# GpSimd's split of a later batch's context, moved from between the fourth and fifth sums of exponentials to behind a batch's last sum

## The chip, the cores and the metric

One core of one Trainium2 chip runs the whole program. The metric is the device time of one execution in microseconds (us), lower being better; the value given for a kernel is the median of its runs.

## The reference

The inputs are 32 sequences of 256 tokens with 256 features, and for each a context of 256 tokens. The reference applies three blocks, each followed by `x = layernorm(x + block(x))`:

```python
x = _layernorm(x + _L0_attn_ref(x, ...))             # 4 layers: sLSTM over 256 steps + feed-forward
x = _layernorm(x + _L0_xattn_ref(x, ctx_1024, ...))  # cross-attention, 16 heads of 64
x = _layernorm(x + _L0_ffn_ref(x, ...))              # ternary weights, 8-bit activations
...
def _L0_xattn_ref(x, context, mask, Wq, Wkv, Wo, bo):
    q = x @ Wq
    k, v = jnp.split(context @ Wkv, 2, axis=-1)
    sim = jnp.einsum('bhid,bhjd->bhij', q, k) * SCALE
    sim = jnp.clip(jnp.where(mask, sim, max_neg), -5.0, 5.0)
    attn = jax.nn.softmax(sim, axis=-1)
    out = jnp.einsum('bhij,bhjd->bhid', attn, v)
    return out @ Wo + bo
```

The change lies in the part that computes the cross-attention and the last feed-forward block. The context enters only through `k` and `v`.

## The kernel before, in words

The kernel has two stages. The first (`slstm`, to about 2220 us of the profile) runs the recurrence. The second (`attend_and_feed`) runs over 32 batches `j`, one sequence each. Every engine has its own list of instructions for the whole stage, written out by hand in program order, and works through it in that order; semaphores alone tie the lists together.

For each batch TensorE first computes 12 units of keys, queries and values (`unit`, L835 for keys and queries, L842 for values), and between them the first half of the feed-forward block of the batch before (`transpose_x`, L920; `feed_in`, L938). Inputs and weights are held as two fp16 numbers, a high part and the rest, and each product is three matmuls. Then come four quads of four heads each. For quad `q` TensorE computes scores of pairs of heads (`scores`, L857), exponentials times values (`attend`, two halves, L867), and the sums of the exponentials (`denominators`, L879); from the second quad on it also multiplies the quad before by `Wo` (`out_project`, L911, 6 matmuls for a pair of heads). Behind the last quad come the last two pairs of `out_project`. `transpose_h` (L948) and `feed_out` (L957) of the batch before stand in quads 2 and 3.

VectorE clips the scores (`clip`, L1175, two heads at a time, into the buffer `scores`), divides (`attended`, L1260), writes the low parts of keys and queries (L1246), quantises (`round_up`, L1227: `gate<-hidden_f`; `round_down`, L1231: `hidden_quant<-gate`), and prepares the x of batch j+2 in pieces: `x1_moments` (L1287, L1290), `x1_centre` (L1296), `x1_residual` (L1305), `x1_second_norm` (L1315, two instructions, one for each half of the tokens). In each batch `attended` of quad 0 is followed by the `round_up` of the second half of the tokens, and then by the clips of heads 8 and 9; `attended` of quad 3 follows `x1_second_norm`; then come `last_attended_lo` (L1267), `fed` (L1273) and `x_plus_attended` (L1463). ScalarE takes the exponentials (L1027), the high parts (L1059, L1063, L1080, L1090) and the logarithm and exponential of the denominators (L1071, L1073).

GpSimd has this list for a batch `j`: `add_halves` for each of 16 heads (L771), which adds the exponentials of the two halves of the context and waits for ScalarE's exponentials of that head; between the fourth and the fifth of them `context_split(j + 2)`; `attended_lo` of quads 0, 1 and 2 (L775) behind heads 7, 11 and 15; in batch 0 alone `below_half` (L780, part of the ternary weights) behind heads 5, 9 and 13; and last `residual(j + 2)` (L765), which waits for VectorE's `x_plus_attended` of batch j. `context_split(n)` waits for the load of batch n and for all 12 units of batch n-2, whose slot it writes; then it writes the high part of the context (L757, a cast) and the low part (L759, a subtraction) into `batch_inputs_hi` and `batch_inputs_lo`. TensorE waits for both only at unit 0 of batch n (`in_split`).

The DMA queue of SyncE loads batch n (`load`, L725 to L728) once `in_split` of batch n-2 and `x1_step` of batch n-1 have come; in its list this load stands behind the store of the result of batch n-4.

The two waits of TensorE that GpSimd can end are these:

```python
def denominators(j, q):
    pe.wait_ge(halves_added, 4 * (n + 1))
def out_project(j, pair):
    pe.wait_ge(ot_split, QUADS * j + pair // 2 + 1)
```

Of the kernel before, what the change touches and what calls it, by code (L numbers as in the profile page):

```python
# [15 lines left out]
B, S, D = 32, 256, 256  # L16
# [569 lines left out]
def attend_and_feed(nc, ctx, a, x4, out, kept):  # L586
# [128 lines left out]
    with nc.Block() as block:  # L715

        @block.sync
        def _(sp):
            def load(n):

                i = n % SLOTS
                if n >= SLOTS:
                    sp.wait_ge(x1_step, X1_OPS * (n - 1))
                    sp.wait_ge(in_split, 2 * (n - 1))
                sp.dma_start(x4t[:, i], token_rows(x4, FIRST, n)).then_inc(in_loaded[i], DMA)  # L725
                if n >= SLOTS:
                    sp.dma_start(xt[:, i], token_rows(a["x"], 0, n)).then_inc(in_loaded[i], DMA)
                    sp.dma_start(cb[:, i], a["ctx"][:, :, n]).then_inc(in_loaded[i], DMA)  # L728

            def store(f):  # L730

                if f > 0:
                    sp.wait_ge(out_stored, f * STORE)
                sp.sem_inc(result_free, 1)
                for tt in range(QT):
                    sp.wait_ge(res_done, f * QT + tt + 1)
                    sp.dma_start(out[f:f + 1, tt * P:(tt + 1) * P, :].rearrange("o t d -> t (o d)"),
                                 res[:, f % SLOTS, tt]).then_inc(out_stored, DMA)

            load(0)  # L740
            load(1)
            for j in range(B):
                if j + 2 < B:
                    load(j + 2)
                if j > 0:
                    store(j - 1)
            store(B - 1)
            sp.wait_ge(out_stored, B * STORE)

        @block.gpsimd  # L750
        def _(pool):
            def context_split(n):
                i = n % SLOTS
                pool.wait_ge(in_loaded[i], LOADS2 * DMA * (n // SLOTS + 1))
                if n > 1:
                    pool.wait_ge(unit_ready, UNITS * (n - 1))
                nc.gpsimd.tensor_copy(xc_hi[:, i, 1], cb[:, i]).then_inc(in_split, 1)  # L757
                pool.wait_ge(in_split, 2 * n + 1)
                nc.gpsimd.tensor_tensor(xc_lo[:, i, 1], cb[:, i], xc_hi[:, i, 1], ALU.subtract).then_inc(in_split, 1)  # L759

            def residual(n):
                pool.wait_ge(x1_step, X1_OPS * (n + 1))
                if n > 1:
                    pool.wait_ge(xa_done, QT * (n - 1))
                nc.gpsimd.tensor_tensor(x1b[:, n % SLOTS], x1[:], bo[:, None, :].broadcast_to([P, QT, D]), ALU.add).then_inc(x1_bo_done, 1)  # L765

            def add_halves(j, i):
                pool.wait_ge(exp_done, AHEADS * j + i + 1)
                if QUADS * j + i // 4 > 1:
                    pool.wait_ge(den_ready, QUADS * j + i // 4 - 1)  # L770
                nc.gpsimd.tensor_tensor(psum[:, i % RING, :], pr[:, i % RING, 0:S], pr[:, i % RING, S:2 * S], ALU.add).then_inc(halves_added, 1)  # L771

            def attended_lo(j, q):
                pool.wait_ge(ot_hi_done, QUADS * j + q + 1)
                nc.gpsimd.tensor_tensor(ot_lo[:, 2 * q:2 * q + 2, :], ot[:, q % 2], ot_hi[:, 2 * q:2 * q + 2, :],  # L775
                                        ALU.subtract).then_inc(ot_split, 1)

            def below_half(m):
                pool.wait_ge(ff_op, 3)
                nc.gpsimd.tensor_scalar(ff_t[:, m, :], ff_raw[:, m, :], ff_minus_half[:, m:m + 1], None, ALU.is_lt).then_inc(ff_below, 1)  # L780

            context_split(0)
            nc.gpsimd.memset(onesf[:], 1.0).then_inc(ones_ready, 1)
            nc.gpsimd.memset(onesb[:], 1.0).then_inc(ones_ready, 1)
            pool.wait_ge(ones_ready, 2)
            for i_, o_ in ((identf, onesf), (identb, onesb)):
                nc.gpsimd.affine_select(out=i_[:], in_=o_[:], compare_op=ALU.is_equal, fill=0.0, base=0,
                                        pattern=[[1, P]], channel_multiplier=-1).then_inc(ident_ready, 1)
            context_split(1)
            pool.wait_ge(w_loaded, DMA * kept["loads"])  # L790
            residual(0)
            residual(1)
            pool.wait_ge(wo_split, 2)
            for j in range(B):
                for i in range(AHEADS):
                    add_halves(j, i)
                    if i == 3 and j + 2 < B:
                        context_split(j + 2)
                    if i % 4 == 3 and i > 3:
                        attended_lo(j, i // 4 - 1)  # L800
                    if j == 0 and i % 4 == 1 and i > 3:
                        below_half(i // 4 - 1)
                if j + 2 < B:
                    residual(j + 2)

        @block.tensor
# [726 lines left out]
```

## Time and profile before

| | before |
|---|---|
| median of 3 runs | 3738.53 us (3736.28 to 3739.94) |
| the profiled execution, its own time | 3732.63 us |
| span of the profiled execution | 3730.9 us |
| granted TensorE clock, mean | 0.99 |
| TensorE busy | 3615.0 us (97%) |
| VectorE busy | 3460.5 us (93%) |
| ScalarE busy | 3064.7 us (82%) |
| GpSimd busy | 2253.7 us (60%) |

The profile is of one execution. Times in it are from the start of the span. In a timeline a row is one instruction or several alike in a row (xcount), its first number is the start and its second the duration of all of them; in square brackets stands how long the engine was idle before it and who ended that. PE is TensorE's matmuls and PEld its weight loads, DVE is VectorE, ACT ScalarE and POOL GpSimd.

### The profile page before, as it was taken

Reading aid. Unit: us, or ns where it says so; the run is one execution under the profiler, and the core shown is the slowest. Engines: PE = TensorE matmul, PEld = TensorE weight load, DVE = VectorE, ACT = ScalarE, POOL = GpSimd, SP = SyncE. Lnnn points to the kernel's source line nnn. Section 1 sums busy time; section 2 is a strip of 40 time slices with the busy share of each in tenths; the row PEclk is TensorE's granted clock in tenths of the full one; section 3 lists DMA queues with packets and bytes.
Section 4 is the critical chain, followed back from the end, with each engine's and each line's share of the span. In section 5 each row is a group of like instructions: output and inputs, shape, how many; then the busy total and the mean of one; then the engine's idle time right before and its main releaser. Section 6 shows DMA issues by size and latency. Waiting matters only on the chain. (4 is left out here: it accounts for less than half of the span.)

```text
span 3730.9 us, 167466 instructions
## 1 busy us (share of the span) xinstructions
PE 3615.0 (97%) x71481; PEld 2282.1 (61%) x71481; DVE 3460.5 (93%) x9241; ACT 3064.7 (82%) x6357; POOL 2253.7 (60%) x2395
## 2 busy tenths in 40 slices
PE   6999999999999999999999987999999999999997
PEld 3666666665666666666666654666666666666664
DVE  8999999999999999999999987889988898888886
ACT  4999999999999999999999984677776677777675
POOL 3777777777777777777777764444444444444442
PEclk9999999999999999999999998999999999999998
DMA  2000221000000000000000000000000000100000
GB/s 82 25 25 25 56 59 53 25 25 25 25 25 25 25 25 25 25 25 25 25 25 25 25 26 18 24 24 24 24 24 24 24 24 28 32 24 24 24 16 10
DMA packets 99973, 104.27 MB, mean 28 GB/s; under 512 B 17297, under 2 KB 95005, under 8 KB 98729
## 3 DMA queue, kind: packets, MB, share of 16 engines
q1 hardware_dynamic: 99224, 93.56, 8.7%
q8 instruction: 560, 9.18, 1.0%
q14 instruction: 189, 1.54, 0.1%
HBM read 48.52 MB, written 17.53 MB: 18 GB/s over the span
## 5 line engine op out<-in xcount | busy, mean ns | idle before, releaser
L565 POOL TENSOR_TENSOR conv_products<-normed_features,conv_taps_by_token 128x256 f32<-128x256 f32 (+1 forms) x837 | 757.9, 919 | 530.2 <-ACT normed_features L348 530.1
L771 POOL TENSOR_TENSOR exps_of_both_halves<-scores 128x256 f32<-128x256 f32 x512 | 424.2, 851 | 583.8 <-ACT scores L1027 578.4
L295 PE MATMUL banks<-up_centred,after_cell_features 128*32 128x336 f32 x8928 | 740.3, 449 | 1.1 <-ACT after_cell_features L348 0.5
L295 PEld LDWEIGHTS banks<-up_centred,after_cell_features 128*32 128x32 f32 x8928 | 260.5, 109 | 277.6 <-issue 224.1
L302 PE MATMUL banks<-down,hidden_features 112*32 112x256 f32 x6696 | 419.2, 383 | 0.0
L578 POOL TENSOR_TENSOR conv_partial_sums<-conv_products,conv_partial_sums 128x512 f32<-128x512 f32 x279 | 370.5, 1328 | 21.9
L1027 ACT ACTIVATE scores<-scores 128x512 f32<-128x512 f32 x512 | 305.4, 626 | 77.7 <-DVE scores L1175 74.0
L366 ACT ACT_TABLE_LOAD x279 | 358.0, 1283 | 5.2
L381 ACT ACT_TABLE_LOAD x279 | 358.0, 1283 | 5.1
L1175 DVE SCALAR_TENSOR_TENSOR scores<-banks,score_top 128x512 f32<-128x512 f32 x512 | 327.9, 681 | 26.1 <-PE banks L857 25.5
L269 PE MATMUL banks<-recurrent_weights,h_features 64*32 64x256 f32 x8928 | 313.1, 379 | 0.3 <-DVE h_features L509 0.2
L867 PE MATMUL banks<-scores,v_tokens 128*32 128x256 f32 x4096 | 274.0, 385 | 11.9 <-ACT scores L1027 11.7
L579 POOL TENSOR_TENSOR conv_partial_sums<-conv_products,conv_partial_sums 128x256 f32<-128x256 f32 x279 | 265.1, 950 | 0.0
L302 PEld LDWEIGHTS banks<-down,hidden_features 112*32 112x32 f32 x6696 | 189.0, 109 | 121.3
L571 POOL TENSOR_TENSOR conv_partial_sums<-conv_products,conv_partial_sums 128x256 f32<-128x256 f32 x279 | 220.3, 790 | 65.9 <-DVEq L466 44.0
L835 PE MATMUL banks<-batch_inputs_hi,qkv_weights_hi 128*128 128x256 f16 x1024 | 196.0, 273 | 11.3 <-POOL batch_inputs_lo L759 9.8
L269 PEld LDWEIGHTS banks<-recurrent_weights,h_features 64*32 64x32 f32 x8928 | 196.1, 106 | 8.3 <-DVE h_features L509 1.5
L835 PE MATMUL banks<-batch_inputs_lo,qkv_weights_hi 128*128 128x256 f16 x1024 | 196.0, 273 | 0.0
L835 PE MATMUL banks<-batch_inputs_hi,qkv_weights_lo 128*128 128x256 f16 x1024 | 195.9, 273 | 0.0
L867 PEld LDWEIGHTS banks<-scores,v_tokens 128*32 128x32 f32 x4096 | 120.9, 110 | 107.6 <-ACT scores L1027 27.1
L269 PE MATMUL banks<-gate_weights,convolved_features 64*32 64x128 f32 x8928 | 186.2, 275 | 0.0
L503 DVE SCALAR_TENSOR_TENSOR convolved_features<-tanh_half_conv,conv_partial_sums 128x256 f32<-128x256 f32 x279 | 180.0, 645 | 0.5 <-ACT tanh_half_conv L365 0.5
(222 smaller groups left out, 9933.3 us busy)
## 6 DMA issues: line engine op xcount, KB each, us to landing
layer_inputs<-layer_outputs SPq DMA_DIRECT2D x279, 96.0 KB, 2.0
layer_inputs<-in_x SPq DMA_DIRECT2D x280, 32.0 KB, 1.8
x_scratch<-layer_outputs SPq DMA_DIRECT2D x279, 32.0 KB
x_tokens<-in_x SPq DMA_DIRECT2D x32, 256.0 KB, 3.0
context_features<-in_ctx SPq DMA_DIRECT2D x32, 256.0 KB, 3.7
layers_out<-x_scratch SPq DMA_DIRECT2D x32, 256.0 KB, 2.8
out<-result SPq DMA_DIRECT2D x64, 128.0 KB, 1.8
up_centred<-in_ff_up SPq DMA_DIRECT2D x1, 2688.0 KB
```

Source lines behind the costliest of these rows:

```text
L269: mm = nc.tensor.matmul(bank[group(l), 2 * (j % 2) + odd, at + g0 * DH:at + g1 * DH], src[r, n, group(l)], w[r, l, n, g0:g1, :].rearrange( ...
L295: mm = nc.tensor.matmul(bank[group(l), b, 0:UP], xmt[:, n, group(l)], up[:, l, n, at:at + UP], start=n == 0, stop=n == HALF - 1, skip_grou ...
L302: mm = nc.tensor.matmul(bank[group(l), FD, 0:D], hidt[:, i, group(l)], down[:, l, i, :], start=i == 0, stop=i == UTILES - 1, skip_group_ch ...
L366: nc.scalar.preload_act_table_set(LOG_EXP)
L381: nc.scalar.preload_act_table(ACT.Gelu)
L565: return nc.gpsimd.tensor_tensor(prod[:, i:i + n], xnt[:, j % NRING].rearrange("p n t -> p (n t)")[:, None, :].broadcast_to([P, n, HALF * ...
L578: nc.gpsimd.tensor_tensor(new[:, 0:2], prod[:, 0:2], old[:, 1:3], ALU.add).then_inc(conv_done, 1)
L771: nc.gpsimd.tensor_tensor(psum[:, i % RING, :], pr[:, i % RING, 0:S], pr[:, i % RING, S:2 * S], ALU.add).then_inc(halves_added, 1)
L835: mm = nc.tensor.matmul(bank[:, b, i * S:(i + 1) * S], w_[:, m, h, (2 * n + i) * P:(2 * n + i + 1) * P], x_[:, j % SLOTS, src, h, :], star ...
L867: mm = nc.tensor.matmul(bank[32 * g:32 * g + 32, b, at:at + S], stationary(kt, i), pr[:, i % RING, kt * S:(kt + 1) * S], start=kt == 0, st ...
L1027: nc.scalar.activation(pr[:, i % RING, :], pr[:, i % RING, :], ACT.Exp, scale=S_SCALE).then_inc(exp_done, 1)
L1175: nc.vector.scalar_tensor_tensor(out=pr[:, i % RING, :].rearrange("p (k s) -> p k s", k=KT), in0=bank[:, i % SCORES, :].rearrange("p (k s) ...
```

## The change

GpSimd's call of `context_split(j + 2)` leaves its place between `add_halves(j, 3)` and `add_halves(j, 4)` and stands behind the whole loop over the heads, ahead of `residual(j + 2)`. Its two instructions and its waits are the same. It is called in the same 30 batches (j = 0 to 29); in batches 30 and 31 it is called in neither kernel.

```diff
             for j in range(B):
                 for i in range(AHEADS):
                     add_halves(j, i)
-                    if i == 3 and j + 2 < B:
-                        context_split(j + 2)
                     if i % 4 == 3 and i > 3:
                         attended_lo(j, i // 4 - 1)
                     if j == 0 and i % 4 == 1 and i > 3:
                         below_half(i // 4 - 1)
                 if j + 2 < B:
+                    context_split(j + 2)
                     residual(j + 2)
```

## Rows read from the trace of the kernel before

**Rows 1.** The page: the chain that ended last, shares by engine

```profile
PE 33%; DVE 4%; ACT 2%; issue 1%; POOL 0%; DMA 0%; DVEq 0%; POOLq 0%
```

**Rows 2.** Chain that ended last, pieces of 60 key and query matmuls: start us, us, what

```profile
3564.73 6.55 PE banks L835 x60
...
3609.51 6.55 PE banks L835 x60
...
3654.48 6.55 PE banks L835 x60
```

**Rows 3.** Waits, 3563 to 3608 (batch 29): us in total, times, longest us

```profile
PEld banks L879 <- POOL exps_of_both_halves L771: 0.2, 1, 0.2
...
PEld banks L911 <- POOL attended_lo L775: 0.4, 1, 0.4
```

**Rows 4.** Timeline of GpSimd, batch 16: start us, us, engine line op, shapes, xcount [idle before]

```profile
3004.97 0.61 POOL L757 CAST batch_inputs_hi<-context_features 128x512 f16<-128x512 f32 x1
...
3005.66 1.49 POOL L759 TENSOR_TENSOR batch_inputs_lo<-context_features,batch_inputs_hi 128x512 f16<-128x512 f32 x1
...
3020.12 1.35 POOL L775 TENSOR_TENSOR attended_lo<-attended,attended_hi 128x512 f16<-128x512 f32 x1
...
3027.70 1.27 POOL L765 TENSOR_TENSOR x_plus_bo<-x_tokens,bo 128x512 f32<-128x512 f32 x1 [6.23 <-DVE x_plus_attended L1463]
```

**Rows 5.** Timeline of VectorE, the same batch

```profile
3007.81 0.69 DVE L1260 TENSOR_TENSOR attended<-banks,denominator_log 128x512 f32<-128x512 f32 x1 [0.23 <-ACT denominator_log L1073]
...
3008.42 0.74 DVE L1227 TENSOR_SCALAR gate<-hidden_f,quant_scale 128x1024 f32<-128x1024 f32 x1
...
3009.08 1.28 DVE L1175 SCALAR_TENSOR_TENSOR scores<-banks,score_top 128x512 f32<-128x512 f32 x2
...
3021.97 0.74 DVE L1315 TENSOR_SCALAR x_tokens<-x_tokens,x_mean_var,x_rstd 128x256 f32<-128x256 f32 x2 [0.64 <-ACT x_rstd L1086]
...
3022.68 0.69 DVE L1260 TENSOR_TENSOR attended<-banks,denominator_log 128x512 f32<-128x512 f32 x1
...
3024.07 0.69 DVE L1267 TENSOR_TENSOR attended_lo<-attended,attended_hi 128x512 f16<-128x512 f32 x1 [0.70 <-ACT attended_hi L1080]
```

**Rows 6.** Timeline of TensorE, the same batch

```profile
3015.43 0.28 PE L857 MATMUL banks<-q_hi,k_hi 64*128 64x256 f16 x2 [0.17 <-DVE scores L1175]
...
3025.29 0.27 PE L911 MATMUL banks<-wo_hi,attended_hi 128*128 128x256 f16 x1
```

**Rows 7.** Groups of VectorE by line and form, 2357 to 3607: busy us, mean ns

```profile
L1227 DVE TENSOR_SCALAR gate<-hidden_f,quant_scale 128x1024 f32<-128x1024 f32 x56 | 42.6, 760 | 0.0
```

**Rows 8.** Timeline of GpSimd, batch 30, which has no split

```profile
3635.84 0.72 POOL L771 TENSOR_TENSOR exps_of_both_halves<-scores 128x256 f32<-128x256 f32 x1 [1.22 <-ACT scores L1027]
```

**Rows 9.** Timeline of VectorE and (last row) TensorE, batch 30

```profile
3635.33 0.69 DVE L1260 TENSOR_TENSOR attended<-banks,denominator_log 128x512 f32<-128x512 f32 x1 [0.23 <-ACT denominator_log L1073]
...
3635.94 1.18 DVE L1227 TENSOR_SCALAR gate<-hidden_f,quant_scale 128x1024 f32<-128x1024 f32 x1
...
3637.03 1.27 DVE L1175 SCALAR_TENSOR_TENSOR scores<-banks,score_top 128x512 f32<-128x512 f32 x2
...
3637.77 0.28 PE L857 MATMUL banks<-q_hi,k_hi 64*128 64x256 f16 x2 [0.36 <-DVE scores L1175]
```

**Rows 10.** Timeline of VectorE and (last row) GpSimd in batch 0: operations that overlap

```profile
2291.70 1.38 DVE L1296 SCALAR_TENSOR_TENSOR layers_out<-layers_out,x_mean_var,post_scale 128x256 f32<-128x256 f32 x1
...
2302.45 1.05 DVE L1315 TENSOR_SCALAR x_tokens<-x_tokens,x_mean_var,x_rstd 128x256 f32<-128x256 f32 x1 [0.60 <-ACT x_rstd L1086]
...
2291.41 1.38 POOL L775 TENSOR_TENSOR attended_lo<-attended,attended_hi 128x512 f16<-128x512 f32 x1
```

**Rows 11.** Timeline of GpSimd and (last row) TensorE in batch 0

```profile
2271.85 0.60 POOL L757 CAST batch_inputs_hi<-context_features 128x512 f16<-128x512 f32 x1
...
2273.64 1.42 POOL L771 TENSOR_TENSOR exps_of_both_halves<-scores 128x256 f32<-128x256 f32 x2
...
2281.92 1.08 PE L879 MATMUL banks<-exps_of_both_halves,ones_for_sums 128*32 128x256 f32 x8 [4.50 <-POOL exps_of_both_halves L771]
```

## The prediction

> **What bounds the kernel now.** I began with the chain that ended last. TensorE holds 33% of it against 4% for VectorE and none for GpSimd [rows 1], and in the second stage it goes through TensorE from batch to batch: one batch begins 44.78 us behind the other [rows 2]. So a change on GpSimd counts only where it moves TensorE. Next I read the waits of one batch. TensorE's list waits for GpSimd at two places, the sums of quad 1 and the first low part of the attended values, for 0.2 and 0.4 us [rows 3], and both are weight loads that stood still while their matmul row had no idle time of its own. Then I laid the timelines of the three engines of batch 16 side by side. GpSimd spends from 3004.97 to 3007.15 on the split [rows 4]. At the end of the batch it has nothing to do for 6.23 us until the residual, which waits for VectorE [rows 4]. VectorE has no idle time from 3007.81 to the second norm at 3021.97 [rows 5], and TensorE waits for it at 3015.43 [rows 6]. Within a batch the score part is thus a loop of TensorE and VectorE, and each tenth that VectorE loses between 3007.81 and 3015.4 goes to TensorE.
>
> **What is moved.** Two GpSimd instructions, 0.69 us from start to start and 1.49 for the second (2.2 us together), in 30 batches; no DMA and no work is added. The queues it passes: the context load of batch j+2 was issued a batch earlier, and the next load that waits for the split stands in SyncE's list behind a store of a later batch, so no transfer moves; its reader on TensorE comes more than a batch later. Behind the new place stands only the residual. The split would run from about 3021.4 (end of the last low part, 3020.12 + 1.35) to about 3023.5, and the residual starts at 3027.70 [rows 4]: it is hidden there, and costs GpSimd's own list nothing. If that cover went, it would cost up to 2.2 us a batch.
>
> **What the old place gives back.** The sums of heads 4 to 7 run when their exponentials come. TensorE gains at most its two waits, 0.6 us a batch [rows 3]; I take nothing, because no matmul stood idle for them.
>
> **Term 1, the sums in their new time.** GpSimd and VectorE hold each other up where VectorE reads two operands from SBUF or runs a scalar operation there: the same 128x256 scalar instruction that takes 0.37 us (0.74 for two) [rows 5] took 1.05 in batch 0, where GpSimd was at a low part [rows 10]. So it matters which pairs meet. Batch 30 has no split, and up to its first `attended` it is what every batch becomes. Counted from that `attended`, VectorE's clips of heads 8 and 9 begin 1.27 us later in batch 16 (3007.81 to 3009.08) [rows 5] but 1.70 us later in batch 30 (3635.33 to 3637.03) [rows 9]. Between them stands `gate<-hidden_f`: 0.74 us with the split [rows 5], 1.18 without [rows 9], because a sum of GpSimd has begun 0.10 us before it [rows 8]. In 28 batches with the split the 56 instructions of this form have a mean of 760 ns [rows 7], so none is held up. TensorE pays at once: its scores of heads 10 and 11 wait 0.36 us in batch 30 [rows 9]. Batch 30 lasts 44.97 us, 0.19 longer than batch 29, though VectorE has no x of a later batch to prepare [rows 2]. In batches 1 to 29 VectorE stays busy until the clip for which TensorE waits at 3015.43, so nothing takes the loss up: 29 x 0.43 = 12.5 us. Bounds: 0.36 us (TensorE's wait in batch 30) to 0.6 (should another instruction meet a sum), 10 to 17 us.
>
> **Term 2, the split in its new time.** No batch shows a split there, so I use the nearest overlap. VectorE's second norm is two scalar instructions at 3021.97 and about 3022.3 [rows 5]. The split's low part is ready 0.69 us behind the cast's start at about 3021.43, at 3022.12: between the two. In batch 0 a low part of the same size became ready at 2291.41, and the second instruction of a pair, from 2291.70, took 1.38 us [rows 10]. I take the second norm's second instruction as held so: 1.3 for 0.37, 0.95 us more. `attended` of quad 3 (3022.68) and `last_attended_lo` (3024.07 to 3024.76) [rows 5] go back with it, the latter to an end at 3025.71. TensorE's matmul that needs it stands at 3025.29 [rows 6]: 0.53 us of slack are used up and about 0.45 remain. 29 x 0.45 = 13 us. Bounds: nothing, if the low part comes after both instructions; and 1.1 us a batch, if both are held (0.7 us more by the other row, 1.05 against 0.37 [rows 10]): 0 to 32 us. The middle is taken since the same size of GpSimd instruction and the same pair of VectorE did this.
>
> The Trainium skill says in its page "SBUF — State Buffer", section "SBUF: two separate sides", that the port pair which VectorE and GpSimd share is a lock that whoever starts first holds for its whole instruction. This trace lets go sooner: VectorE's instruction ends at 2293.08, only 0.29 us behind the end of GpSimd's at 2292.79 [rows 10]. By the page, the second norm would end a whole 0.37 us behind the low part, some 0.1 us more a batch, and the sum would come to 28 us.
>
> **Batch 0.** There GpSimd is the bound: TensorE stood 4.50 us before the sums of quad 1 [rows 11]. The sums of heads 4 and 5 can begin where the cast did, 1.8 us earlier (2271.85 for 2273.64) [rows 11]. At the end of the batch the split meets VectorE's x and its last ternary weights, and most of this may be lost: -1.8 to 0, I take -0.5.
>
> **Sum.** 12.5 + 13 - 0.5 = 25 us. The profiled execution of before took 3732.6 us, 0.16% under the median of the runs, and would take 3757.6; against the median, 3763.5.
>
> **Rivals.**
> Only term 1: GpSimd's low part slips behind both instructions of the second norm, or the slack of 0.53 us holds. For it: 0.18 us later is enough to slip. Against it: both overlaps of rows 10 held VectorE. 3738.5 + 12 = 3750.5 us.
> Both terms larger: both instructions of the second norm are held, 12.5 + 32 - 0.5 = 44, 3782.5 us. The first starts 0.07 us before the cast's end, so it could be.
> Nothing moves: the waits that appear have slack that I missed. Against it: the wait of 0.36 us in batch 30. 3738 us.
> Faster: VectorE's loop gains. The split goes from beside `hidden_quant` ahead of 3007.81, GpSimd lags less, and if `gate<-hidden_f` isn't caught, TensorE's wait at 3015.43 (0.17 us) goes, 5 us in 29 batches, with 1.8 in batch 0: 3731.7 us. It decides from the point where the sum of head 6 begins over 0.1 us later than in batch 30, behind `gate<-hidden_f`.
> That the change doesn't do what it says can't be here: GpSimd's list runs in the written order.
>
> **How the numbers follow.** The forecast has 0.62, only term 1 0.18, larger 0.06, nothing 0.09, faster 0.05. A measurement of this kernel can tell about 0.2%, 7.5 us, from no change; both the forecast and the case of term 1 alone lie above it. Faster 0.05, same 0.09, slower 0.86. The range goes from the case of term 1 alone to the forecast with some of term 2's upper bound: 3749 to 3772.
>
> **What would show it.** `gate<-hidden_f` of the second half at 1.18 us in batches 1 to 29, and the mean of the 56 at about 970 ns; TensorE idle 0.36 us before the scores of heads 10 and 11; the second norm's pair at about 1.7 us for 0.74; TensorE waiting about 0.45 us for VectorE before `out_project` of pair 6; 45.65 us from batch to batch, and 1.8 us less at the sums of quad 1 in batch 0. A period of 45.2 would leave term 2 wrong, one of 44.8 or less the whole argument.

## The result, and the profile after

| | before | after |
|---|---|---|
| median | 3737.7 us (4 runs) | 3755.0 us (4 runs, 3752.9 to 3756.5) |
| the profiled execution | 3732.6 us | 3755.1 us |
| from batch to batch, most batches | 44.78 us | 45.52 us |

The change makes the kernel slower: the ratio of after to before is 1.0045 (95% interval 1.0028 to 1.0063), 17 us. In the code of after all lines behind the moved call stand one line earlier (L1227 is now L1226, L1315 is L1314, and so on).

The page of after, its first line and the chain by engine; TensorE's share was 33% [rows 1]:

```profile
span 3753.3 us, 167466 instructions
...
PE 27%; DVE 6%; ACT 4%; issue 3%; POOL 0%; DMA 0%; DVEq 0%; POOLq 0%
```

The chain that ended last, in order of time (start us, us, what), where batches 29, 30 and 31 begin:

```profile
3586.76 6.55 PE banks L834 x60
...
3632.27 6.55 PE banks L834 x60
...
3677.24 6.55 PE banks L834 x60
```

Batch 29 lasts 45.51 us where it lasted 44.78; batch 30, in which neither kernel splits a context, lasts 44.97 in both [rows 2]. So the loss is in the batches with a split, and is the same in each: from batch 2 on they last 45.51 to 45.53 us, but for batch 13, which is 0.35 us longer in both kernels. In the kernel before one batch, number 28, lasted 45.38 us (more on it below).

The timeline of VectorE in batch 16, the rows that answer to [rows 5] (start us, us, engine, line, operation, shapes, xcount, idle before):

```profile
3020.82 0.69 DVE L1259 TENSOR_TENSOR attended<-banks,denominator_log 128x512 f32<-128x512 f32 x1 [0.23 <-ACT denominator_log L1072]
...
3021.43 1.18 DVE L1226 TENSOR_SCALAR gate<-hidden_f,quant_scale 128x1024 f32<-128x1024 f32 x1
...
3022.53 1.27 DVE L1174 SCALAR_TENSOR_TENSOR scores<-banks,score_top 128x512 f32<-128x512 f32 x2
...
3035.41 1.58 DVE L1314 TENSOR_SCALAR x_tokens<-x_tokens,x_mean_var,x_rstd 128x256 f32<-128x256 f32 x2 [0.64 <-ACT x_rstd L1085]
...
3036.91 0.68 DVE L1259 TENSOR_TENSOR attended<-banks,denominator_log 128x512 f32<-128x512 f32 x1
...
3038.28 0.69 DVE L1266 TENSOR_TENSOR attended_lo<-attended,attended_hi 128x512 f16<-128x512 f32 x1 [0.70 <-ACT attended_hi L1079]
```

`gate<-hidden_f` takes 1.18 us for 0.74, and the clips behind it begin 1.71 us after `attended` for 1.27: 0.44 us lost. The pair of the second norm takes 1.58 us for 0.74: 0.84 us lost. The second instruction of the pair by itself:

```profile
3035.74 1.25 DVE L1314 TENSOR_SCALAR x_tokens<-x_tokens,x_mean_var,x_rstd 128x256 f32<-128x256 f32 x1
```

GpSimd's timeline of the same batch:

```profile
3021.33 1.87 POOL L771 TENSOR_TENSOR exps_of_both_halves<-scores 128x256 f32<-128x256 f32 x2 [1.22 <-ACT scores L1026]
...
3034.86 0.61 POOL L757 CAST batch_inputs_hi<-context_features 128x512 f16<-128x512 f32 x1
...
3035.55 1.29 POOL L759 TENSOR_TENSOR batch_inputs_lo<-context_features,batch_inputs_hi 128x512 f16<-128x512 f32 x1
...
3041.45 1.27 POOL L765 TENSOR_TENSOR x_plus_bo<-x_tokens,bo 128x512 f32<-128x512 f32 x1 [4.61 <-DVE x_plus_attended L1462]
```

The sums of heads 6 and 7 now begin 0.10 us ahead of `gate<-hidden_f` (3021.33 against 3021.43), as in batch 30 of the kernel before [rows 8]. The split's cast starts at 3034.86, its low part at 3035.55, between the two instructions of the second norm (3035.41 and 3035.74), and the second of them ends at 3036.99, 0.15 us behind the low part's own end. The residual still waits 4.61 us for VectorE: in GpSimd's own list the split is hidden. The context load that SyncE issues in this batch comes 10.96 us after the batch's start, where it was 10.98 before, so it didn't move.

TensorE's timeline of the same batch, its two waits for a clip and the two matmuls on either side of its new wait:

```profile
3023.26 0.28 PE L856 MATMUL banks<-q_hi,k_hi 64*128 64x256 f16 x2 [0.37 <-DVE scores L1174]
...
3028.87 0.28 PE L856 MATMUL banks<-q_hi,k_hi 64*128 64x256 f16 x2 [0.17 <-DVE scores L1174]
...
3038.62 0.27 PE L910 MATMUL banks<-wo_hi,attended_lo 128*128 128x256 f16 x1
...
3039.03 0.28 PE L910 MATMUL banks<-wo_hi,attended_hi 128*128 128x256 f16 x1
```

It waits 0.37 us before the scores of heads 10 and 11, where batch 16 of before had no wait, then 0.17 as before [rows 6]. The last two rows are the end of pair 5 and the start of pair 6 of `out_project`: 0.41 us apart where two matmuls in a row stand 0.11 apart, so 0.30 us lost. With the 0.44 us that the clips come later this makes the 0.74 of the period.

The groups by line and form from batch 2 to 29 (busy us, mean ns, idle before):

```profile
L1226 DVE TENSOR_SCALAR gate<-hidden_f,quant_scale 128x1024 f32<-128x1024 f32 x56 | 54.0, 965 | 0.0
...
L1314 DVE TENSOR_SCALAR x_tokens<-x_tokens,x_mean_var,x_rstd 128x256 f32<-128x256 f32 x56 | 44.1, 830 | 17.9 <-ACT x_rstd L1085 17.9
```

The mean of `gate<-hidden_f` went from 760 [rows 7] to 965 ns, that of the second norm from 410 to 830: every batch is alike.

Batch 0 in before: the residual of batch 1 on GpSimd's timeline, which shows how late the second stage was, and the start of batch 1 in the chain. Below it the same two rows of after, and between them TensorE's first matmuls of the sums of quad 1:

```profile
2267.86 1.27 POOL L765 TENSOR_TENSOR x_plus_bo<-x_tokens,bo 128x512 f32<-128x512 f32 x1 [24.56 <-DVE x_tokens L1315]
...
2309.95 6.55 PE banks L835 x60
```

```profile
2268.59 1.27 POOL L765 TENSOR_TENSOR x_plus_bo<-x_tokens,bo 128x512 f32<-128x512 f32 x1 [23.31 <-DVE x_tokens L1314]
...
2280.85 0.64 PE L878 MATMUL banks<-exps_of_both_halves,ones_for_sums 128*32 128x256 f32 x8 [2.74 <-POOL exps_of_both_halves L771]
...
2310.38 7.99 PE banks L834 x60
```

This execution of after came 0.73 us later into batch 0 (2268.59 for 2267.86), and still had the sums of quad 1 1.07 us earlier (2280.85 for 2281.92 [rows 11]), so the freed place gave 1.8 us. At the start of batch 1 it was 0.43 us later (2310.38 for 2309.95), and 0.73 of lateness less 0.43 leaves 0.3 us of the gain, by one profile of each kernel. Then the first 60 matmuls took 7.99 us for 6.55. Stretches of 2310 to 2318 us, busy time of each engine, then the granted clock (0.80) and DMA; first before, then after:

```profile
2310.00:2318.00 8.00, 8.00 (x76) 7.08 (x74) 7.47 (x22) 4.97 (x10) 1.27 (x1) 1.00 0.00 0
```

```profile
2310.00:2318.00 8.00, 8.00 (x61) 6.59 (x60) 5.96 (x19) 4.06 (x7) 1.27 (x1) 0.80 0.00 0
```

The 0.80 is a mean: TensorE was granted 0.50 (1.2 GHz) from 2310 to 2312 us, 0.70 from 2312 to 2314 and 1.00 (2.4 GHz) from then on, where the kernel before had 1.00 throughout. In both kernels it had stood idle for over 5 us before the last sums of batch 0 (5.41 us, and 5.14 before). The experiments show below that this loss comes and goes.

### The profile page after: what moved, and what is told of

Read it like the earlier page. It is cut to its first block and busy times, and to the rows that moved or that the text cites. A ratio compares the mean times of both kernels' runs of the same rounds, so it can differ in the third digit from the quotient of the medians.

```text
span 3753.3 us, 167466 instructions
## 1 busy us (share of the span) xinstructions
PE 3623.8 (97%) x71481; PEld 2280.2 (61%) x71481; DVE 3486.8 (93%) x9241; ACT 3064.8 (82%) x6357; POOL 2256.6 (60%) x2395
## 5 line engine op out<-in xcount | busy, mean ns | idle before, releaser
L771 POOL TENSOR_TENSOR exps_of_both_halves<-scores 128x256 f32<-128x256 f32 x512 | 431.9, 864 | 649.5 <-ACT scores L1026 646.2
```

## The experiments

The theory was that two overlaps of GpSimd and VectorE cost: a sum that now holds `gate<-hidden_f`, and the split's low part that holds the second norm. I give the time from batch to batch for most batches from the chain of each profile, since it repeats to 0.01 us, and the ratio to the kernel before of the same chip beside it. Chips differ: the kernel before had medians of 3731.95, 3737.73 and 3730.68 us on the three chips on which most of the experiments ran.

### The split behind the residual

```diff
                 if j + 2 < B:
-                    context_split(j + 2)
                     residual(j + 2)
+                    context_split(j + 2)
```

> The changed kernel with the split one step later, behind the residual. Theory (two overlaps cost: a sum of GpSimd holds VectorE's gate<-hidden_f 0.43 us, and the split's low part holds the second norm 0.84 us, of which 0.53 are slack): the second goes, the first stays. gate<-hidden_f still 1.18 us, the second norm's pair back at 0.74, no wait of TensorE before out_project of pair 6, 45.2 us from batch to batch (45.52 in the changed kernel, 44.8 before), about 3746 us. Rival (the split delays the residual and with it the batch's end): the residual is now ahead, all is back, 44.8 and 3738 us. Rival (the split costs wherever it stands ahead of a batch's first sum): 45.5, 3755 us.

Measured: 45.44 us from batch to batch, ratio 1.0050 (1.0034 to 1.0067). This is a miss: the second norm is free, but the batch is only 0.08 us shorter than in the changed kernel, close to the second rival's 45.5. The starts of batches 3 and 4 in the chain, and the groups of `x2` (written `x`) and of the second norm:

```profile
2397.74 6.55 PE banks L834 x60
...
2443.18 6.55 PE banks L834 x60
...
L1189 DVE TENSOR_SCALAR x<-x_plus_attended,mean_var,rstd 128x256 f32<-128x256 f32 x52 | 40.7, 825 | 0.0
...
L1314 DVE TENSOR_SCALAR x_tokens<-x_tokens,x_mean_var,x_rstd 128x256 f32<-128x256 f32 x52 | 19.1, 411 | 16.6 <-ACT x_rstd L1085 16.6
```

The second norm is back at 411 ns, but `x` of the batch before, a pair of the same kind that takes 405 ns in the other kernels, now takes 825: the split meets it at the start of the next batch. The kind of overlap is that of the theory, but I had not looked at what stands at the place to which I moved the split. The pair is held for 0.84 us as the second norm was, and 0.22 us of it reach the period (45.44 against the 45.22 of the next experiment). They do so at two waits of TensorE's weight loads, for `x_quant` and for `hidden_f`, both of which VectorE reaches later after it was held:

```profile
2995.34 0.11 PEld L919 LDWEIGHTS banks<-identity_bf,x_quant 128*128 128x128 bf16 x2 [0.18 <-DVE x_quant L1230]
...
2999.63 0.11 PEld L937 LDWEIGHTS banks<-ff_ternary,x_quant_features 128*128 128x128 bf16 x2 [0.47 <-DVE hidden_f L1250]
```

With the pair free (the kernel with the second norm moved, below) the first of these waits is absent and the second is 0.20 us. Laid over that kernel's batch 16, TensorE's matmuls come 0.08 us later from the first place on and 0.22 from the second.

### No split at all

```diff
                 if j + 2 < B:
-                    context_split(j + 2)
+                    pool.wait_ge(unit_ready, UNITS * (j + 1))
+                    pool.sem_inc(in_split, 2)
                     residual(j + 2)
```

It leaves out the fp16 parts of the contexts of batches 2 to 31.

> The changed kernel without the split for batches 2 to 31 (they use the context's fp16 parts of batches 0 and 1; only the semaphore is raised), 60 GpSimd instructions less. Theory: slower than before although work is gone, since gate<-hidden_f meets a sum as in batch 30: 45.2 us from batch to batch, about 3746 us, and 1.18 us for gate<-hidden_f. Rival (it is the split's own time at the new place that costs): 44.8 or less, 3737 us or less.

Measured: 45.22 us, ratio 1.0030 (1.0019 to 1.0040), as the theory had it. Without 60 instructions of GpSimd the kernel is slower than with them at the old place. The group of `gate<-hidden_f`:

```profile
L1227 DVE TENSOR_SCALAR gate<-hidden_f,quant_scale 128x1024 f32<-128x1024 f32 x53 | 51.0, 962 | 0.0
```

The mean is that of the changed kernel. This is the first overlap alone, 0.43 us a batch: the split between the fourth and the fifth sum had kept the later sums late enough for `gate<-hidden_f` to pass.

### `gate<-hidden_f` of the second half ahead of `attended` of quad 0

```diff
+                    if j > 0 and s_ == 1:
+                        h_round_up(f, 1)
                     if s_ % 2 and q + 1 < QUADS:
                         attended(j, q)
...
-                        if s_ == 1:
-                            h_round_up(f, 1)
```

> The changed kernel with VectorE's gate<-hidden_f of the second half ahead of attended of quad 0 in place of behind it, so that it begins about 0.8 us ahead of the sum of head 6. Theory: it takes 0.75 us, partly in VectorE's idle 0.23 us, and the first term goes: the second norm still 1.58, 45.52 - 0.43 - 0.1 = 45.0 us from batch to batch, about 3740 us. Rival (the first term is not this overlap, but the earlier sums and low parts as such): the time stays at 45.5, 3755 us.

Measured: 44.88 us, ratio 1.0008 (0.9998 to 1.0017). Groups of `gate<-hidden_f` and of the second norm:

```profile
L1226 DVE TENSOR_SCALAR gate<-hidden_f,quant_scale 128x1024 f32<-128x1024 f32 x54 | 40.5, 749 | 0.0
...
L1314 DVE TENSOR_SCALAR x_tokens<-x_tokens,x_mean_var,x_rstd 128x256 f32<-128x256 f32 x52 | 41.0, 832 | 16.6 <-ACT x_rstd L1085 16.6
```

The first overlap is gone and the second is there. The batch is 0.64 us shorter than in the changed kernel, more than the 0.43 of the overlap and the 0.1 that I had added. The instruction now fills VectorE's idle 0.23 us, and less of the held norm comes through. TensorE's rows of batch 16, its one wait, and the end of pair 5 and the start of pair 6:

```profile
3010.91 1.07 PE L866 MATMUL banks<-scores,v_tokens 128*32 128x256 f32 x16 [0.54 <-DVE attended L1259]
...
3027.04 0.27 PE L910 MATMUL banks<-wo_hi,attended_lo 128*128 128x256 f16 x1
...
3027.30 0.28 PE L910 MATMUL banks<-wo_hi,attended_hi 128*128 128x256 f16 x1
```

The last two are 0.26 us apart, so 0.15 us are lost there and not 0.30.

### The second norm behind `attended` of quad 3

```diff
-                        if s_ == 7:
-                            x1_second_norm(later)
...
                 attended(j, QUADS - 1)
+                if later:
+                    x1_second_norm(later)
                 last_attended_lo(j)
```

> The changed kernel with the second norm behind attended of quad 3 in place of ahead of it, where VectorE is idle for 0.70 us. By then the split's low part is over. Theory: the second norm's pair takes 0.74, attended of quad 3 starts where it did before, TensorE's wait before out_project of pair 6 goes, gate<-hidden_f stays at 1.18: 45.2 us from batch to batch, about 3746 us. Rival (TensorE's late out_project comes from GpSimd's list, not from the second norm): 45.5, 3755 us.

Measured: 45.22 us, ratio 1.0027 (1.0015 to 1.0038), as expected. The same two groups:

```profile
L1226 DVE TENSOR_SCALAR gate<-hidden_f,quant_scale 128x1024 f32<-128x1024 f32 x53 | 51.0, 962 | 0.0
...
L1314 DVE TENSOR_SCALAR x_tokens<-x_tokens,x_mean_var,x_rstd 128x256 f32<-128x256 f32 x52 | 18.9, 406 | 0.0
```

Now the first overlap is there and the second is gone: 0.30 us a batch.

### The same move in the kernel before

The diff is the one above, on the kernel before.

> The kernel before with the second norm behind attended of quad 3. Theory: with no split there the norm is not held, and its 0.74 us fit into idle time of VectorE at either place: 44.78 us from batch to batch, as before. So the gain of this move in the changed kernel is the overlap, not the move. Rival (the move is a gain by itself): 44.5.

Measured: 44.79 us, ratio 1.0002 (0.9992 to 1.0012). The move is worth nothing where the split does not meet the norm, so what it gained in the changed kernel was the overlap.

### The split at both places

```diff
                 if j + 2 < B:
+                    context_split(j + 2, True)
                     residual(j + 2)
```

on the kernel before, with the counts of `in_split` raised to match.

> The kernel before with the split done twice, at the old place and again behind the batch's last sum (the same values are written again; the counts of in_split are raised to match). Theory: the old place keeps gate<-hidden_f at 0.75 us, the new one holds the second norm: 44.78 + 0.31 = 45.1 us from batch to batch, 29 x 0.31 = 9 us over the kernel before, although GpSimd does 2.2 us more a batch than in the changed kernel, which takes 45.52. Rival (what costs is GpSimd's work in the scores as such): slower than the changed kernel, over 45.6.

Measured: 45.09 us in most batches, ratio 1.0030 (1.0019 to 1.0042). Four starts in the chain, of batches 12 and 13 and of batches 15 and 16, and the two groups:

```profile
2809.23 6.55 PE banks L839 x60
...
2854.32 6.55 PE banks L839 x60
...
2944.84 6.55 PE banks L839 x60
...
2990.53 6.55 PE banks L839 x60
...
L1231 DVE TENSOR_SCALAR gate<-hidden_f,quant_scale 128x1024 f32<-128x1024 f32 x52 | 42.5, 818 | 0.0
...
L1319 DVE TENSOR_SCALAR x_tokens<-x_tokens,x_mean_var,x_rstd 128x256 f32<-128x256 f32 x52 | 41.0, 830 | 16.6 <-ACT x_rstd L1090 16.6
```

GpSimd does more than in either kernel, and the batches are shorter than in the changed one: not GpSimd's work costs, but which instruction of VectorE it meets. Six batches, as the one from 2944.84 to 2990.53, lasted 45.7 us: here `gate<-hidden_f` is held after all (its mean is 818 and not 750 ns). More on this below.

### Both moves of VectorE

The two diffs of VectorE above together, on the changed kernel.

> The changed kernel with both moves on VectorE: gate<-hidden_f of the second half ahead of attended of quad 0, and the second norm behind attended of quad 3. Theory: the two overlaps are independent, so the gains add: 45.52 - 0.64 (44.88 with the first alone) - 0.30 (45.22 with the second alone) = 44.58 us from batch to batch, 0.2 under the kernel before, 29 x 0.2 = 6 us less than it, a ratio of 0.9985. Rival (one overlap hides behind the other): 44.8 or more, no faster than before.

Measured: 44.71 us, 3728.9 us against 3737.7 of the kernel before on the same chip, ratio 0.9977 (0.9967 to 0.9986). It is faster than both kernels, but by less than these medians say: 0.07 us in an ordinary batch, and 1341.3 us for 1344.5 from the start of batch 1 to that of batch 31. The other 5 to 6 us of the 8.8 aren't in the batches of the two profiles (see the sum, below). The start of batches 16 and 17 in the chain and TensorE's one wait in the batch:

```profile
2982.21 6.55 PE banks L834 x60
...
3026.93 6.55 PE banks L834 x60
...
3009.21 1.07 PE L866 MATMUL banks<-scores,v_tokens 128*32 128x256 f32 x16 [0.54 <-DVE attended L1259]
```

The sum of the two gains would have given 44.58. The wait in the last row is longer than in the changed kernel (0.54 us for 0.37), since `attended` of quad 0 now stands behind `gate<-hidden_f`. But the kernel with the first move alone has the same wait (3010.91 above), so it is in its 44.88 already and isn't what is missing. What is missing is the second gain: with the first move made, the held norm cost TensorE 0.15 us and not 0.30, and freeing it gave 0.17 (44.88 less 44.71). So the two gains aren't independent: part of the one loss hides behind the other's wait.

### The move of `gate<-hidden_f` in the kernel before

> The kernel before (the split between the fourth and the fifth sum) with gate<-hidden_f of the second half ahead of attended of quad 0. Theory: there the sums of heads 4 to 7 run from 7.1 to 10.4 without a break, so gate<-hidden_f, about 7.55, meets one and waits up to 0.3 us, which uses VectorE's idle 0.23: 44.7 to 44.9 us from batch to batch, no gain by this alone. Rival (the move on VectorE is a gain by itself, whatever GpSimd does): 44.78 - 0.2 = 44.58, as in the kernel with both moves.

The diff is that of `gate<-hidden_f` above, on the kernel before.

Measured: 44.86 us, ratio 0.9990 (0.9981 to 0.9999). The ordinary batch loses 0.08 us: `gate<-hidden_f` now meets a sum here (its mean is 824 ns), and TensorE waits 0.68 us for `attended`. The move pays only where the split is out of the way. That the timed runs are 0.1% faster all the same isn't in the ordinary batches; its profile has no batch of 45.4 us, of which the kernel before has some (below), but whether that is the cause stays open.

### The split behind the sixth sum

```diff
-                    if i == 3 and j + 2 < B:
+                    if i == 5 and j + 2 < B:
                         context_split(j + 2)
```

> The kernel before with the split between the sixth and the seventh sum, in place of between the fourth and the fifth. Theory: the split's cast follows the sum of head 5 at about 7.3 and its low part runs from 8.0 to 9.15, so gate<-hidden_f, from 8.4 (times within the batch as in batch 16, 3000 taken off), waits for it for about 0.6 us: about 1.3 us for 0.75, and 45.3 to 45.5 us from batch to batch. Rival (GpSimd's work is hidden anywhere between the sums, only the place behind the last sum costs): 44.8.

Measured: 45.06 us, ratio 1.0027 (1.0016 to 1.0038). The direction is right, the size was put at twice what it is. The split's low part on GpSimd, and then `gate<-hidden_f` on VectorE:

```profile
3013.57 1.16 POOL L759 TENSOR_TENSOR batch_inputs_lo<-context_features,batch_inputs_hi 128x512 f16<-128x512 f32 x1
```

```profile
3014.25 1.02 DVE L1227 TENSOR_SCALAR gate<-hidden_f,quant_scale 128x1024 f32<-128x1024 f32 x1
```

I had let VectorE wait until the low part's end at 3014.73. But `gate<-hidden_f`, which needs 0.75 us alone, ended at 3015.27 and so, as an estimate, began its work at 3014.52, 0.95 us after the low part's start.

### The kernel before and the changed kernel, once more

> The changed kernel itself, once more beside the kernel before, for the size of the whole effect: 45.52 us from batch to batch again. Theory: 29 batches x 0.74 us = 21.5 us, less 0.3 us in batch 0, a ratio of 1.0057 to the kernel before; if the 1.4 us that TensorE lost at its low clock at the start of batch 1 belongs to the change it is there again, if it is chance it is not.

Measured: 45.52 us again, 3753.8 us, ratio 1.0043 (1.0030 to 1.0056). The first 60 matmuls of batch 1 took 6.79 us, so of the 1.4 us lost to the low clock 0.24 were left: it is no part of the change. Other kernels had 6.55 to 8.18 us there.

> The kernel before itself, profiled once more. Its first profile took 3732.6 us where the median of its runs is 3737.7. Theory (the batches are alike in every run and the difference lies in the first stage and in TensorE's clock around batch 0): 44.8 us from batch to batch again, and more time ahead of batch 2. Rival (the first profile was of a faster phase of the batches): 44.9 to 45.0 from batch to batch, and the change's real cost is 0.55 us a batch and not 0.74.

Measured: 44.78 us, with two batches of 45.37 and 45.38; ratio to itself 0.9999. Neither theory holds as I put it: the batches are alike, and this execution, of 3732.1 us on another chip, was as short as the first. The medians of the kernel before go by chip (3730.7 us here, 3737.7 on the chip of the changed kernel's second profile); what differs between the chips isn't shown.

> The kernel before itself once more. In its two profiles nearly all batches last 44.78 us, but three of them 45.38, and there gate<-hidden_f is held by a sum; in the others it begins 0.06 us ahead of it. Theory (a batch of the kernel before can fall on either side of this edge, and how many do differs from execution to execution): the batches are again of 44.78 or 45.38 us and no other length but the one or two that any kernel has, and the span goes with the count of the long ones, 0.6 us each. Rival (all runs alike): the count is the same, two at most, and the 4 to 7 us between the chips come from elsewhere.

Measured: 44.78 us, no batch of 45.38, and the shortest span of the three (3727.8 us for 3730.9 and 3730.3, with one and two such batches). So the number of them does differ from run to run, by 0.6 us each, but it is too small to explain several us. This is the long batch in the first profile of before, VectorE's `gate<-hidden_f` and the sum of GpSimd beside it, and then the sum of batch 16, where `gate<-hidden_f` is not held [rows 5]:

```profile
3545.78 1.35 DVE L1227 TENSOR_SCALAR gate<-hidden_f,quant_scale 128x1024 f32<-128x1024 f32 x1
```

```profile
3545.84 0.74 POOL L771 TENSOR_TENSOR exps_of_both_halves<-scores 128x256 f32<-128x256 f32 x1
```

```profile
3008.48 1.27 POOL L771 TENSOR_TENSOR exps_of_both_halves<-scores 128x256 f32<-128x256 f32 x1
```

In both batches the sum starts 0.06 us behind `gate<-hidden_f`. Once VectorE takes 0.74 us and the sum 1.27; once VectorE is held and takes 1.35, and the sum 0.74. The kernel before stands on an edge, the changed kernel clearly on the wrong side of it, by 0.10 us.

## Why the prediction was right

**The bound, and GpSimd's list.** Right: the split is hidden in GpSimd's own list (the residual waits 4.61 us), the load did not move, and nothing was gained from the old place in batches 1 to 29: the two waits of TensorE's weight loads [rows 3] are gone, and the period has both losses in full.

**Term 1.** Right, to the hundredth: 0.43 us a batch, with 0.37 us of waiting on TensorE and the mean of 965 ns that was forecast as 970. It is also what is left without any split (45.22 us), and goes when `gate<-hidden_f` is moved out of the sum's way. One reading on the way was wrong: of the 56 instructions with the mean of 760 ns [rows 7] I said that none is held, and one was, that of batch 28 with 1.35 us; the others take 749. I had read an edge as a safe distance.

**Term 2.** The mechanism was right, the size was not: I took 0.95 us for the second norm and 0.45 for TensorE (0.95 less the slack of 0.53 is 0.42), and it was 0.84 and 0.30. The step that was off is what the held instruction loses: I took it to last 1.3 us for 0.37, from a `layers_out` row, and it lasts 1.25 for 0.41. Of the 0.84 us, 0.77 reach `last_attended_lo` (2.87 us behind the second norm for 2.10), and TensorE's matmul begins 0.06 us behind its end (3038.97 and 3039.03), so the slack was 0.47 and not 0.53. A tenth in what overlaps is a quarter of what comes through behind a slack of half a us. The held instruction ended at 3036.99; it needs 0.41 us alone, so by this estimate it began its work at 3036.58, 0.26 us before the low part's own end at 3036.84. The Trainium skill has the shared ports locked for the whole of the instruction that came first (page "SBUF — State Buffer", section "SBUF: two separate sides"). By the rows the trace differs, as it did in batch 0 of before: here, and with the split behind the sixth sum, VectorE is let go 0.2 to 0.3 us before GpSimd's row ends.

**Batch 0.** 0.3 us gained in one pair of profiles, 0.5 taken, with the 1.8 gained first and lost at the end as said.

**The sum.** 25 us were forecast and 17 measured, inside the range. Taken from the traces the cost is 0.74 x 29 = 21.5 us, less 0.3; the smaller term 2 explains the difference of this to 25. The two profiled executions differ by 22.4 us (3755.1 and 3732.6), and their chains account for it: 21.5 us, with 1.4 for the low clock at the start of batch 1 and less 0.6 for the long batch of before. Another 4 to 5 us, between these 21 and the 16 to 17 of the medians (3755.0 less 3737.7, 3753.8 less 3737.7), stay open. The kernel before seems to be what is slow there. On the chip where its median was 3737.7, the medians set it 5 to 6 us further behind the kernel with both moves than the batches of the profiles do, and about 4 us behind the one with the move of `gate<-hidden_f` alone, though only 1 to 3 us in the comparison with the kernel with the split at both places. On the chip where its median was 3732.0 such gaps are at most about 2 us. The long batches go the right way, since the changed kernel has none, but I saw at most two in one execution (1.2 us), and no profile of before was taken on the chip where it was slowest.

**The rivals.** Nothing moves and faster are out. Only term 1 is out: the norm is held in every batch. That both instructions of the norm are held is out too; the first one takes 0.41 us.

## What to carry to other kernels

In this kernel an instruction of GpSimd costs what it takes from the instruction of VectorE that it meets, and removing one can make the kernel slower, because all that follows on GpSimd comes earlier and meets something else. Before moving work on GpSimd, lay its new times beside VectorE's list and mark the operations with two SBUF inputs and the scalar operations on SBUF data; a batch or an iteration that lacks the moved step already shows the first half of the result. Look at the new place as closely as at the old one, and at the edge: here, where two starts lay 0.06 us apart, the order changed from one iteration to the next.

## What the runs showed that I had not expected

- Two starts that are 0.06 us apart in the records can go either way: 0.74 or 1.35 us for `gate<-hidden_f` with the same rows around it.
- The clock of TensorE at the start of batch 1 depends on the execution: the same kernel took 7.99 and 6.79 us for the same 60 matmuls there, and 6.55 is what they take at full clock.
- The slack behind `x` at the start of a batch is smaller than I took it to be: its two instructions were held for 0.84 us together, and 0.22 us of it came through to the batch.
- Two gains that come from separate overlaps didn't add up: 0.64 and 0.30 us alone, 0.81 together.
